# Filler matmuls in the set-up, and the first and last pass of a two-layer decoder kernel drawn up anew

## The reference

```
x = x + mla(layernorm(x))              # L0: latent attention, 16 heads of 16, rotated by head index
x = x + xattn(layernorm(x), ctx)       # L0: 16 heads of 64, softmax over the heads of one token
x = x + mod_ffn(layernorm(x))          # L0: the 128 tokens with the highest router score get a GELU ffn, added to the normalised rows
x = x + sparse(layernorm(x))           # L1: 16 heads of 16, only the 25 largest scores of a row kept (the others are 0) before softmax
x = x + masked(layernorm(x), ctx)      # L1: attention over the context, keys beyond a length masked
x = x + ternary(layernorm(x))          # L1: weights quantised to -1, 0, 1
```

## Time and profile before

| | us |
|---|---|
| median of 3 runs | 5929.49 |
| lowest, highest run | 5927.11, 5936.82 |
| the profiled execution | 5895.52 |
| its span, first to last instruction | 5893.7 |
| TensorE busy, weight loads busy | 5465.2, 3848.0 |
| VectorE, ScalarE, GpSimd busy | 4493.7, 3735.3, 2278.1 |
| mean granted clock of TensorE, share of full | 0.948 |

### The profile page before, as it was taken

The page is one execution under the profiler, slowest core; times in us unless marked ns, Lnnn a source line. Parts: engine busy times, 40 slices in busy tenths (PEclk is TensorE's granted clock), DMA queues, the critical chain, the costliest instruction groups (busy, mean ns, idle before and its releaser), DMA issues.

```text
span 5893.7 us, 114534 instructions
## 1 busy us (share of the span) xinstructions
PE 5465.2 (93%) x40094; PEld 3848.0 (65%) x40094; DVE 4493.7 (76%) x16125; ACT 3735.3 (63%) x9377; POOL 2278.1 (39%) x4100
## 2 busy tenths in 40 slices
PE   7899999999999999999999999999999999999987
PEld 4666666666666666666666666666666666666654
DVE  2577897777787778787786887777897777888683
ACT  3566676666666666667665666666676666676542
POOL 0233443334443434444333444333444333443341
PEclk7899999999889999899999999899999999999876
DMA  2000000000000000000000000000000000000000
GB/s 90 6 5 5 9 8 9 5 8 7 7 8 6 8 8 5 8 8 8 5 8 5 9 8 8 5 7 7 9 8 8 5 8 7 7 8 8 1 5 6
DMA packets 29347, 53.06 MB, mean 9 GB/s; under 512 B 8145, under 2 KB 9810, under 8 KB 27986
## 3 DMA queue, kind: packets, MB, share of 16 engines
q1 hardware_dynamic: 28770, 45.73, 2.5%
HBM read 37.33 MB, written 8.39 MB: 8 GB/s over the span
## 4 chain that ended last, share of the span: by engine, by line
PE 69%; DVE 13%; ACT 11%; issue 3%; POOL 3%; ACTq 0%; DVEq 0%; POOLq 0%
PE bankH L738 8%; PE bankM L554 6%; PE bankM L495 6%; DVE wk L1073 4%; PE bankH L761 4%; PE bankM L581 4%; PE bankT L495 3%; PE bankT L596 3%; PE bankM L476 3%; PE bankH L778 3%; DVE m L1069 3%; PE bankM L468 2%; PE bankM L551 2%; DVE m_nm L505 2%; ACT m_pT L568 2%
## 5 line engine op out<-in xcount | busy, mean ns | idle before, releaser
L1073 DVE MATCH_REPLACE8 wk<-m,wk 128x256 f32<-128x256 f32 x2048 | 820.4, 407 | 0.0
L1069 DVE MAX8 m<-wk 128x8 f32<-128x256 f32 x2048 | 756.7, 410 | 0.0
L1094 POOL TENSOR_SCALAR mx<-m 128x2 f32<-128x2 f32 x512 | 115.1, 225 | 1651.1 <-DVE wk L1073 1646.3
L505 DVE TENSOR_REDUCE m_nm<-bankM 128x2 f32<-128x512 f32 x1024 | 657.9, 679 | 109.9 <-PE bankM L495 108.4
L1103 POOL TENSOR_TENSOR t_pr<-wk,sc 128x256 f32<-128x256 f32 x1024 | 728.8, 733 | 1.3 <-PE bankT L596 1.3
L1106 POOL TENSOR_TENSOR t_pr<-t_pr,sc 128x256 f32<-128x256 f32 x1024 | 727.8, 732 | 0.0
L836 ACT ACTIVATE xk_area<-bankH,xb 64x256 f32<-64x256 f32 x1024 | 480.1, 469 | 176.0 <-PE bankH L738 158.6
L554 PE MATMUL bankM<-m_q,m_kT 32*128 32x512 f32 x2048 | 582.6, 649 | 0.0
L495 PE MATMUL bankM<-m_kT,m_q 32*128 32x256 f32 x4096 | 534.0, 399 | 16.8 <-DVE x L689 8.9
L1030 ACT ACTIVATE t_pr<-t_pr,t_nm 128x256 f32<-128x256 f32 x1024 | 470.5, 513 | 36.3 <-POOL t_pr L1106 31.8
L605 ACT ACTIVATE t_pt<-bankT 128x512 f32<-128x512 f32 x512 | 309.9, 605 | 237.6 <-PE bankT L596 229.4
(11 more groups left out here) (224 smaller groups left out, 11849.9 us busy)
## 6 DMA issues: line engine op xcount, KB each, us to landing
xin<-x_in SPq DMA_DIRECT2D x32, 256.0 KB, 2.6
ctxA<-ctx_in SPq DMA_DIRECT2D x32, 256.0 KB, 2.6
ctxB<-ctx_in SPq DMA_DIRECT2D x32, 256.0 KB, 2.6
out<-x SPq DMA_DIRECT2D x32, 256.0 KB, 2.0
w<-w_w SPq DMA_DIRECT2D x2, 1024.0 KB
xwq<-w_xwq SPq DMA_DIRECT2D x1, 1024.0 KB
xwk<-w_xwk SPq DMA_DIRECT2D x1, 1024.0 KB
xwv<-w_xwv SPq DMA_DIRECT2D x1, 1024.0 KB
```

The lines of the kernel that those rows point to most:

```text
L505: nc.vector.tensor_reduce(b["nm"][:, i % 2, 2 * (i // 2) + x, :], banks[u % 4][:].rearrange("p (j s) -> p j s", j=2), AX.X, ALU.max, negat ...
L1069: link.inc(nc.vector.max(top, src[:, t, :]))
L1073: m = nc.vector.match_replace(out=wk[:, k, t, :], in_to_replace=take, in_values=src[:, t, :], imm_value=-BIG)
```

## The change

What the change does:

- In the first block TensorE waits for `ones` and then issues 48 fillers of `ones` by `ones` (WARM).
- `fill` works in the set-up pass too, with fillers of `ones` by `ones` and a table FILL_START: 0 at the latent projection, 3 ahead of the scores of step 2, 3 ahead of step 6, 3 ahead of `shift_rows`, 5 and 5 in part two.
- `tensor_at` gets three more places: ahead of the scores of steps 2 and 6 of part one, and one in a chunk of its own between part one and `shift_rows`, which waits for the 14th maximum. So c has 5 places and m 6, and a lap of c or m has one chunk more on PE (CHUNKS 34 to 35 and 33 to 34).
- The strings ORDER_FIRST and ORDER_LAST are others on all four engines, and FILL_FIRST and FILL_LAST too. The first pass has 102 fillers where it had 33, the last 187 where it had 56, with up to nine at one place.
- In the loop the tables give 0 at the new places, and ORDER["pe"] differs by one letter m or c a lap for the new chunk. The strings of ACT, DVE and POOL stay.

The diff, of each long string its first line alone:

```
 ORDER_FIRST = {
     "pe": runs("""
-        h4 m h4 m h2 m h m h m h2 m h2 m2 h2 m2 h m3 h m h m h3 m2 h3 m2 h2 m h m h3 m2 h2 m h3 m3 h t m h m h m h m h m2 h13 m h5 t h t h t h t
+        h m h6 m h2 m h4 m2 h2 m h m h m h2 m h2 m h2 m h m h2 m2 h2 m h m h2 m h3 m h m h2 m2 h t h m h2 m h4 m3 h m h m2 h3 m h7 m h5 t h
...
+WARM = 48
+FILL_START = {"m": ["033355"]}
-        "c": ["31", "23", "30", "20"],
-        "m": ["110", "001", "110", "010"]}
-FILL_FIRST = {"t": ["02221000"],
-        "h": ["21122000220", "22221000002"],
-        "m": ["020", "100"]}
-FILL_LAST = {"t": ["22200100", "22201000", "22222222"],
-        "h": ["12000121000", "22222011000"],
-        "c": ["10", "00", "12", "12"],
-        "m": ["000"]}
+        "c": ["00031", "00023", "00030", "00020"],
+        "m": ["100010", "000001", "100010", "000010"]}
+FILL_FIRST = {"t": ["33812062"],
+        "h": ["21141110900", "05131000900"],
+        "m": ["103826", "473202"]}
+FILL_LAST = {"t": ["18120501", "08822010", "44303533"],
+        "h": ["28150070020", "00841000030"],
+        "c": ["16219", "35831", "00900", "04892"],
+        "m": ["220241"]}
...
+            @block.tensor
+            def _(pe):
+                pe.wait_ge(s_set, 1)
+                for _ in range(WARM):
+                    nc.tensor.matmul(bankT[0][:, 0:P], ones[:], ones[:], start=True, stop=True)
...
         def fill(letter, place, to):
-            if lap["of"] == "all":
-                for _ in range(int(FILLERS[letter][lap["n"] - first[letter]][place])):
-                    nc.tensor.matmul(to, w["xwq"][:, 0, 0:P], w["xwq"][:, 1, 0:P], start=True, stop=True)
+            table = {"start": FILL_START, "all": FILLERS}[lap["of"]]
+            if letter in table:
+                for _ in range(int(table[letter][lap["n"] - first[letter]][place])):
+                    if lap["of"] == "start":
+                        nc.tensor.matmul(to, ones[:], ones[:], start=True, stop=True)
+                    else:
+                        nc.tensor.matmul(to, w["xwq"][:, 0, 0:P], w["xwq"][:, 1, 0:P], start=True, stop=True)
...
                 elif i >= 2:
                     pe.wait_ge(*at(g[n + "_nm"], 2 * i - 2))
+                if i in (2, 6):
+                    fill("c" if masked else "m", i // 4 + (not masked), bankM[2 * i % 4][:, 0:P])
                 at_scores(n, b, [bankM[2 * i % 4], bankM[(2 * i + 1) % 4]], i, masked)
+            yield
+            pe.wait_ge(*at(g[n + "_nm"], 14))
+            fill("c" if masked else "m", 2 + (not masked), bankM[0][:, 0:P])
             yield from shift_rows(pe, n, b, bankM[2])
```

More of the change, by code:

```diff
@@ new lines @@
+        c2 t h c h3 m t c2 t m2 t h2 c m c t h m h2 m2 t h m h t h t m t h m2 h2 m h2 m t m2 t h c m3 t h m3 t m t m2 h t h2 t m3 h8 m h m t h t
+        m h m c t2 m h t m t c h c h t h3 c h t c h2 t h2 t h c t h c t h c h t h t c h t2 c h c2 t h2 t2 c h c h t c h3 c t3 c2 h2 c2 t h2 t h
+        t c t c h c h t h c2 h t2 h c t h c t h c2 h c h t h t h c2 t h2 t2 c t c h t h2 t h4 t c h4 c h c2 t c t c t c2 t c2 t2 c t2 c t2 c t2
+        c2 t3 c t2 c2 t c4 t c t c t c2 t c2 t c3 t2 c t c t3 c2 t c t3 c t5 c33"""),
@@ new lines @@
+    "act": runs("""
+        c h t h3 c t c h t5 h2 t h t h t h t h t c t h4 c h t h2 t4 h t h3 t h t m h t2 h2 t h4 t3 h3 t2 h c3 t3 h c h3 c t4 c t c t c h2 t c t2
+        h2 c2 h t c2 t2 c t h c h t2 h3 c t2 c2 t h2 c h2 t2 h2 t2 h3 c t h m2 h2 t2 m t h2 c h t h m h m t h t c t2 h6 t2 h t3 h2 t h t h t2 h
+        t m3 t h t2 m2 h m2 t3 m t m2 t h2 m3 h m h2 m h m2 t2 m2 h t c t2 c t4 h m h t h t c h t h3 c t h3 t h t h3 t h t3 h3 t h t h t2 h t2 h
+        t h3 t3 h3 t h t3 h2 t2 h3 t2 h3 t h t h3 t h c t2 h4 c t h c t h c t2 h t h c t h2 t2 c h2 c t h3 c t2 c t2 h2 t2 h2 t h c h t c t h2 c
+        h c2 t4 h2 t h3 t h c2 t h t2 c2 t h t c t h t h t h t3 c t2 h t h t h t c2 h3 t h2 c4 t29 c2 t4 c t4 c t3 c2 t c t2 c t2 c t c2 t c t
+        c2 t2 c t4 c4 t3 c t11 c t2 c t9 c t3 c24"""),
@@ L97 @@
+        t3 c m2 t h m2 h t m2 t h m2 t m2 t2 m3 c t m t m t3 m h4 t2 h5 t2 h2 t2 h c t2 c m t m2 c h t2 c m h2 t h t6 c t4 c t c t4 c t c t c t3
+        c2 t2 c t c3 h t2 c2 t h t2 h c h t c h t2 h2 t4 h t h t4 h t2 h t2 h t4 h t h t3 h t h t5 c t c t c t3 h3 c h c3 h6 t c t3 c4 h c h t4
+        c4 t c3 t c t2 c t2 c t4 c t2 c t2 c t4 c t2 c2 t29 c3 t4 c3 t2 c t4 c t6 c t4 c28"""),
     "pool": runs("""
[L98 removed]
@@ L99 @@
-        h t3 h t3 h t h t8 h3 c5 t c t20 c t21 c2 t c t8 c t c6"""),
+        t c h c h c t2 h t7 m h t6 c t6 h t7 h t m t3 h m t3 c h c t3 h t c t c h t h t h t4 m t h2 t3 h t4 h c2 h2 t3 h t18 h c t3 h t2 h t2 h
+        t3 h t4 h t4 h t3 h t4 h t h t2 c3 t h c3 t15 c t24 c t c t4 c t4 c t3 c6"""),
 }
@@ new lines @@
+        h m h t h t h m h t c m t h t c h t m t c h c t h3 c2 h3 c2 h t h c h c h c h2 t c2 h t h c t c h c t c2 h c2 t c h t2 c2 h3 t c4 h t c
+        h c t m2 t c h m h t h c m c h t m h m h t2 h c2 h3 t m2 t m h t h m h t h m h m h m t h t m2 t m2 t m h m h m t m4 t h c t h m t h m3
+        h4 t h3 t h m t h m2 t h2 m t m c m t2 h t h t c h t c h c h c2 h2 t c h c h c h t h c m c h t h2 t c2 h t c h c t h c3 h t c t c h t c3
+        h t h c2 h c2 t h2 t c2 t h t m c h2 m h c t h c h t m t h3 m t h c m c t m t m h2 m2 h t m h t h m h m h m2 t m t m2 t h m h m t m4 t m
@@ L113 @@
+        h m t m2 t m h m2 t h t m t m h6 t h2 t h m"""),
     "act": runs("""
@@ L1135, in tensor_at @@
                 if i in (2, 6):
-                    fill("c" if masked else "m", i // 4 + (not masked), bankM[2][:, S:S + P])
+                    fill("c" if masked else "m", 3 + i // 4 + (not masked), bankM[2][:, S:S + P])
             yield from at_out_pe1(pe, n, b, [bankM[3], bankM[2]], 2)
```

49 lines of the change are left out of this document (16 added, 33 removed).

## The result

| us | before | after |
|---|---|---|
| median of the first comparison, 4 executions each | 5933.05 | 5894.21 |
| lowest, highest of them | 5927.11, 5936.82 | 5876.71, 5899.31 |
| ratio, 95% interval | | 0.993 [0.9907, 0.9953] |
| the profiled execution, its span | 5895.52, 5893.7 | 5899.31, 5897.5 |
| mean granted clock in it | 0.948 | 0.956 |

The first comparison says 39 us faster, and the forecast was 5893.5. But the two profiled executions are level, and that is the first thing a reader should stumble on. An execution over 1.5% above the fastest of its kernel in one comparison is left out of all means and ratios, though not of medians and ranges: one of 6308.40 us, and three just over that line (5972.53 to 5975.23).

What follows compares the result with a forecast made beforehand. TensorE was taken to bound the loop, and a chain between engines at low clock the ends. Block and set-up -4, first pass -12, last pass -20, loop 0: 5929.5 - 36 = 5893.5 us, range 5856 to 5928.

Steps and rivals of the forecast that it cites:

- I carry that over unchanged.: Starting point: the three timed runs lie some 34 us above the profiled 5895.5 us, and this was kept, giving 5929.5.
- First block, "+0.5" and "-1": Block one: 48 fillers close it 0.5 us late; the higher clock in the work after them saves 1 us.
- Set-up pass, -3.5: Set-up pass: part one 0, fillers and faster steps in part two -2, a faster end of the pass -1.5 us.
- I take 0: Set-up, part one: nine fillers hide behind VectorE's maxima at full clock, cost up to 4.5 us at half; priced 0.
- five steps then save 6 us: Set-up, part two: five fillers costing 2.5 us raise the clock, and the five steps behind them save 6 us.
- First pass, -12: First pass: 20 us recovered of a 25 us ceiling, less 8 us for 69 added fillers, half on the path.
- Last pass, -20: Last pass: 36 us recovered of a 42 us ceiling, less 16 us for 131 added fillers, half on the path.
- 10 in all: Last lap of c, part two: each step saves 1.2 us by full clock, 10 us together.
- Loop, 0 ± 15: The loop's 28 laps: same rows, so no change, though clock dips may fall elsewhere, 15 us either way.
- The clock falls again in the waits: Rival, chance 0.16: fillers miss a lone stream's waits, half the ceilings come back: -12 us, 5917 us.
- The loop gives it back: Rival, chance 0.10: the ends gain 36 us, but the loop loses 28 us to its slow pattern: 5922 us.
- Fillers at half clock that do not raise it: Rival, chance 0.12: fillers in the lone laps' part two are paid at half clock without raising it: +25 us, 5954 us.

Runs made afterwards that it cites:

- e1: The kernel before, unchanged, timed and traced again: median 5911.91 us, ratio 0.9997 against itself.
- e3: The changed kernel without the first block's 48 fillers and the set-up pass's 19: 5908.75 us, 0.9986 to before.
- e12: The kernel before with only the first pass's new strings and 102 fillers: 5907.37 us, 0.9971 to before.
- e8: The changed kernel with the three old fillers back in the last lap of c, where it has 23: 5885.50 us, 0.9967 to before.
- e7b: The changed kernel with old last pass, five set-up fillers, nine in c's last lap, six in both lone passes' m_ot wait: 5882.38 us, 0.9943 to before.
- e4: The changed kernel with the last pass's strings and filler table as before: 5898.28 us, 0.9972 to before.
- e5: The changed kernel, unchanged, timed and traced again: 5907.56 us, 0.9981 to before.
- e6: The changed kernel with the 33 old fillers in the first pass, new strings kept: 5925.86 us, 1.0 to before.
- e9: e7b with nine fillers instead of five in the set-up pass: 5862.82 us, 0.9913 to before.
- e2: The changed kernel with first and last pass (strings, filler tables) as before, WARM and FILL_START kept: 5908.31 us, 0.9988 to before.
- e11: e9 without the six fillers in the m_ot wait (GAP_START, GAP_LAST = 0, 0): one execution, 5881.28 us.

## Why the prediction came out, and where it was wrong

The forecast met the first comparison's median within a us, for a reason that is only partly right. By the stages' averages the change is worth -16 in the first pass, +1 in the set-up and +3 in the last pass, -12 us; by all executions -14 ± 13. The forecast's sum was -36, and the draw of the first comparison supplied the rest.

**"I carry that over unchanged."** This step failed first. The profiled execution lay 34 us under the three timed runs because executions of this kernel differ by up to 100 us (5871 to 5973); nothing shows that timed runs are longer. The same kernel's later traced execution (e1) took 5927.4. By the mean of 120 the starting point was 5919.9, and a sum of -36 would have given 5884.

**First block, "+0.5" and "-1": right on its first half.** After's rows:

```profile
1.04 12.48 PE L329 MATMUL bankT<-ones 128*128 128x128 f32 x96 [1.04 <-DVE ones L333]
...
14.60 0.85 DVE L357 MEMSET mask_lhs<- 1x128 bf16 x4
...
18.99 1.12 PE L467 MATMUL bankM<-ident,m_pT 128*128 128x128 f32 x4 [5.47 <-DVE m_pT L457]
...
22.66 2.89 PE L480 MATMUL bankM<-m_pT,wq 128*128 128x256 f32 x8
```

The fillers end at 13.5 us, before VectorE's last constant at 15.4, so they close nothing late. TensorE then idles 5.47 us, not 3, and the clock is at half from 17.8 us on; the projection wins 0.6 us instead of 1.6.

**Set-up pass, -3.5: wrong, measured +1** (84.1 to 92.8, mean 86.9, against 85.8). The pass took 73.3 us at a clock of 0.63 in after's trace, where the forecast named under 67 at above 0.75. Two terms. "I take 0" for nine fillers in part one: they stood on the path at half clock. The spreading began at 45.92 to 48.30 us with them (six traces), and without them at 44.24 to 45.45 (eight): +2.6 us on average. And "five steps then save 6 us": the clock rose behind the first five, and three steps took 2 us each, until the wait of 1.75 us for m_ot:

```profile
58.74 2.50 PE L434 MATMUL bankM<-ones 128*128 128x128 f32 x10
...
63.74 0.39 PE L563 MATMUL bankM<-m_m,sel_b 32*128 32x512 bf16 x2
...
65.67 0.39 PE L563 MATMUL bankM<-m_m,sel_b 32*128 32x512 bf16 x2
...
68.67 0.77 PE L593 MATMUL bankM<-m_pT,m_va 128*32 128x256 f32 x8 [1.75 <-ACT m_ot L600]
69.37 0.61 PE L563 MATMUL bankM<-m_m,sel_b 32*128 32x512 bf16 x2
...
76.62 0.64 PE L593 MATMUL bankM<-m_pT,m_va 128*32 128x256 f32 x8
```

The second five raised it once more, for the last step (0.64 at 76.62). From the spreading to L643 part two took 30.8 to 31.5 us in five of the six traces with these fillers, and 31.5 without any (e3, e12): even. In e8 and e7b the first five did not raise the clock, and e8's part two took 35.3 us. That the pass lost 1 us and not 2.6 is the last projection's doing, which ran at full clock (2.0 us) in e4, e5 and e6. The prediction set the warning of idle gaps in the Trainium skill ("TensorE: Matmul & The Clock Gate", section "Why this matters for your kernels") against the busy stretch at half clock. Its direction fits the traces at 68.67 us here and at 5865.18 in the last lap, but the gaps there, 1.75 and 1.93 us, are shorter than those that the section warns of.

**First pass, -12: right in kind and nearly in size**, -12.7 between the first two traces and -16 between the averages. The stretch at 128.5 is at full clock as forecast (1.00, above). The term "half of 17 us on the path" holds about: TensorE's idle time fell from 33.1 us (283.9 - 250.8) to 25.0 (271.2 - 246.2), and was 33.6 in e6, where only the fillers are the old ones. So some 8 us of the fillers took the place of idle time, and the rest stood on the path.

**Last pass, -20: wrong, measured +3** (584.8 us with the new tables; 495.7 + 86.0 with the old). Most of the miss is in the last lap of c. Of the ceiling of 42 us, 20 were its own, and 85% of them less its 20 fillers makes -14.5; measured is +3.5. "10 in all" by short steps counted eight steps and had three at full clock. The 6 us of the projections came to nothing (3.78 us each, as before), and the 4 us of part one turned into +3.9, with 12 fillers there. Its fillers were priced at 0.25 us, half of them hidden, where the eight and the nine took 0.47 us each (3.78 / 8, 4.21 / 9), mostly in the open. The step itself was well sized (2.1 forecast, 2.02 measured). The same nine fillers with the wait filled give 8.1 us (e7b, e9).

The stage to t's last lap was left some -5 us by the forecast's terms, and measured is 495.3 against 495.7. Its three laps, by t's output projections, before and then after:

```profile
5315.90:5492.80 176.90, 161.26 (x1189) 114.94 (x1189) 139.07 (x498) 114.71 (x289) 71.30 (x128) 0.93 0.02 7
5492.80:5655.30 162.50, 147.57 (x1044) 108.28 (x1043) 127.30 (x480) 103.95 (x265) 69.08 (x122) 0.92 0.01 4
5655.30:5808.20 152.90, 114.31 (x651) 70.36 (x650) 115.11 (x437) 58.49 (x118) 56.82 (x108) 0.69 0.02 4
```

```profile
5312.70:5495.50 182.80, 171.69 (x1335) 124.72 (x1334) 139.71 (x499) 116.46 (x294) 70.92 (x128) 1.00 0.03 7
5495.50:5653.30 157.80, 142.39 (x1093) 108.29 (x1090) 128.59 (x480) 100.40 (x260) 69.19 (x122) 0.98 0.01 5
5653.30:5808.10 154.80, 118.43 (x681) 77.49 (x679) 115.74 (x436) 58.35 (x118) 56.53 (x108) 0.69 0.01 4
```

The stretch at 5685.4, with its ceiling of 11 us, lies in the third lap: the clock there rose from 0.50 to 0.58, but that of the whole lap stayed at 0.69. Nothing was recovered in the lap as a whole, so nothing shows whether VectorE would have held it back. The 45 us that left half clock (147 to 102) were in the first two laps. In this stage less half clock does go with less time: over the nine traces with the old last pass its length is 450.8 us + 0.28 us for each us at half clock (140 to 167 us, correlation 0.98). By that line, drawn out to 102 us, an estimate, the old instructions would take 480 us. The new ones take 495.3, with 164 fillers instead of 53 and 28.5 us more of TensorE's time for them (53.6 less 25.1). In the first lap, with 58 more fillers, the clock is 1.00 and the lap 5.9 us longer; in the second, with 38 more, the lap is 4.7 us shorter. So by this estimate clock was won in this stage and fillers spent it again, about half of their time on the path, as priced. No run separates the fillers of this stage from its new strings.

**Loop, 0 ± 15: the value stands, the bound was too narrow.** Eleven traces with the new ORDER_FIRST average 4960 us there, three with the old 4948, in a spread of 59. They had 299 and 261 us at half clock on average, which by the line above accounts for it. That the loop pays back part of the first pass is not shown and not excluded.

**The rivals.** *The clock falls again in the waits* is what set-up and last lap did; its -12 is what the executions say (-14), though here the first pass gave all and the lone passes nothing. *The loop gives it back* stays open. *Fillers at half clock that do not raise it* is right at single places (the first five in e8 and e7b, after's eight), and wrong as the whole.

## What to carry to other kernels

Before a profiled execution and a few timed runs are compared, find out how much executions of one kernel differ, and in which stage: here one stage held nearly all of it, and short stages read from traces told apart what totals could not. Price clock recovery lap by lap, against the time that the fillers take there, and count only the work up to the next long wait. In the lone laps here fillers paid as a run of nine with six more in the wait behind it. Those on the path that no rise of the clock followed were pure cost.

## What was not expected

- Short runs of fillers are a gamble. In the set-up, the first five fillers (2.50 us) were followed by full clock in five traces (after, e5, e2, e4, e6) and not in e8 and e7b; the second five were in all six that had them. Nine (3.1 to 4.2 us) were followed by it in all three set-ups and all eight last laps that had them. But eight (3.78 us) ahead of the spreading in the last lap were not, in any of four traces, so the number alone does not decide it.
- The clock was lost at short waits: behind 1.75 and 1.93 us idle in after and in e11's set-up, and not behind 0.2 to 0.4 us next to fillers. In e11's last lap the scores behind the 1.93 us still ran at full clock, and the value product after them did not.
- The loop's share at half clock differs by 58 us (256 and 314) between two traces of one kernel, and by up to 146 us (212 to 358) over all, while its work is the same. It costs 0.40 us a us, less than the half that a loop bound by TensorE alone would lose.
